# First feed-forward pass: order of casts, raw weight loads, residual loads and low parts, and two places for raw down-projection weights

## The reference, cut to what matters

```
xn = layer_norm(x, gamma)
h = xn @ Wff1                      # 512 -> 2 * 2048
a, gate = h[..., :2048], h[..., 2048:]
out = out + silu(gate) * a @ Wff2  # 2048 -> 512
x = x + tanh(g_xattn[0]) * out
```

## Time and profile before

| | us |
|---|---|
| median of 3 runs (2460.36 to 2461.43) | 2460.55 |
| the profiled execution | 2449.93 |
| its span in the trace | 2448.1 |
| TensorE matmul busy | 2133.0 (87%) |
| VectorE busy | 1324.5 (54%) |
| ScalarE busy | 674.0 (28%) |
| GpSimd busy | 621.1 (25%) |
| DMA, mean over the span | 231 GB/s |

### The profile page before, as it was taken

One profiled execution on the slowest core, in us unless ns is written; L12 is line 12 of the kernel. 1 busy time (PEld: TensorE's weight loads), 2 busy tenths in 40 slices (PEclk: granted clock), 3 DMA queues, 4 the chain that ended last, 5 costly groups with the idle time before them and its releaser, 6 DMA issues. The chain is left out here.

```text
span 2448.1 us, 30049 instructions
## 1 busy us (share of the span) xinstructions
PE 2133.0 (87%) x11425; PEld 1592.8 (65%) x11425; DVE 1324.5 (54%) x2112; ACT 674.0 (28%) x1066; POOL 621.1 (25%) x552
## 2 busy tenths in 40 slices
PE   6999999999968999999999999999897526434898
PEld 5677777776647778888888888887783102111577
DVE  7655666656325777666766676667661000000377
ACT  2544464446423332111111111222430000000231
POOL 5444564445337861330033000000220000000020
PEclk9999999999979999999999999999998767767999
DMA  4223213321186768774876484443769999999867
GB/s 153 75 100 126 83 61 110 125 82 57 39 327 223 254 215 334 260 235 168 316 247 226 156 332 184 155 156 133 291 242 407 426 432 425 421 429 426 320 226 255
DMA packets 181396, 565.13 MB, mean 231 GB/s; under 512 B 15472, under 2 KB 98960, under 8 KB 152560
## 3 DMA queue, kind: packets, MB, share of 16 engines
q1 hardware_dynamic: 171952, 504.37, 55.3%
q10 hardware_dynamic: 9312, 58.99, 5.8%
HBM read 450.07 MB, written 113.25 MB: 230 GB/s over the span
## 5 line engine op out<-in xcount | busy, mean ns | idle before, releaser
L1368 PE MATMUL ff_down<-w,u 128*128 128x512 f32 x1536 | 369.3, 397 | 15.8 <-DVE ff_x L1642 10.4
L1309 PE MATMUL ff_up<-ff_t,w 128*128 128x512 f32 x1488 | 358.9, 390 | 9.2 <-ACT ff_gate L1441 9.2
L1368 PEld LDWEIGHTS ff_down<-w,u 128*128 128x128 f32 x1536 | 289.3, 190 | 89.7 <-DVE ff_x L1642 24.4
L1309 PEld LDWEIGHTS ff_up<-ff_t,w 128*128 128x128 f32 x1488 | 280.0, 188 | 67.8 <-issue 9.6
L1309 PE MATMUL ff_up<-ff_b,w 128*128 128x512 f32 x1176 | 290.0, 391 | 14.8 <-DMA ff_b<-xnT 14.8
L1309 PEld LDWEIGHTS ff_up<-ff_b,w 128*128 128x128 f32 x1176 | 222.3, 189 | 61.6 <-issue 15.2
L1642 DVE SCALAR_TENSOR_TENSOR ff_x<-ff_down,gates,ff_x 128x512 f32<-128x512 f32 x256 | 190.5, 748 | 96.3 <-PE ff_down L1368 94.2
L2395 PE MATMUL e_down<-e_w,e_ug 128*32 128x512 f32 x480 | 70.3, 739 | 187.1 <-DMA e_w<-in_L_ffn_e_W 187.1
L2395 PEld LDWEIGHTS e_down<-e_w,e_ug 128*32 128x32 f32 x480 | 16.9, 133 | 239.2 <-DMA e_w<-in_L_ffn_e_W 196.2
L2067 POOL TENSOR_TENSOR yn_lo<-y,yn_hi 128x2048 fp32r<-128x2048 f32 x8 | 36.7, 4593 | 440.1 <-ACT yn_hi L2032 440.1
L2497 DVE TENSOR_TENSOR e_u_rows<-e_turned,e_b1T 128x128 f32<-128x128 f32 x16 | 4.7, 292 | 264.0 <-PE e_turned L2386 264.0
(11 more groups left out here) (441 smaller groups left out, 4204.2 us busy)
## 6 DMA issues: line engine op xcount, KB each, us to landing
w<-ff_w_factors SPq DMA_DIRECT2D x48, 1792.0 KB, 7.5
e_w<-in_L_ffn_e_W SPq DMA_DIRECT2D x17, 4096.0 KB, 23.4
e_wg<-in_L_ffn_e_Wg SPq DMA_DIRECT2D x16, 4096.0 KB, 35.6
e_w<-in_L_ffn_e_W ACTq DMA_DIRECT2D x13, 4096.0 KB, 53.0
ff_w_factors<-w SPq DMA_DIRECT2D x16, 1792.0 KB, 6.9
w<-ff_w_parts SPq DMA_DIRECT2D x48, 512.0 KB, 5.1
ff_t<-ff_t_factors SPq DMA_DIRECT2D x16, 1024.0 KB, 15.5
ff_b<-xnT SPq DMA_DIRECT2D x13, 1024.0 KB, 11.1
```

The lines of the kernel that those rows point to most:

```text
L1309: last = nc.tensor.matmul(bank[:, :], a, m, start=start and c == 0, stop=stop and c == 5)
L1368: last = nc.tensor.matmul(DN[m % 2][:, :], a, w, start=c == 0, stop=c == 5)
```

## The change

It touches only `feed_forward`.

- `raw2` and its semaphore become two each, place f % 2.
- SyncE: raw w2 1 is loaded right behind raw w2 0. Behind the factor loads the order becomes: raw 4 (after a wait for `w1_lo` of block 2), keep_w1(2), keep_w2(0), raw w2 2, keep_w1(0), the two x loads, raw 3 (after a wait for `w1_lo` of block 1 and for the first low parts), keep_w1(1), keep_w2(1), raw w2 3. In the loop raw f + 2 goes ahead of keep_w1(f), and raw w2 f + 1 is loaded in place of f.
- ScalarE: high_w2(1) goes ahead of group(1), high_s(1) behind group(2), and finish(2) ahead of high_a(3).
- GpSimd: make_w2(1) goes ahead of sum_w1(3).
- VectorE, in all passes: the residual of tile 2 goes between low_u(n, 1) and low_u(n, 0); the residuals behind `finish` begin with tile 3.

```diff
-        raw2 = mem.sbuf("ff_raw_w2", [P, D])
+        raw2 = [mem.sbuf(f"ff_raw_w2_{i}", [P, D]) for i in range(2)]
@@ sync
             load_raw2(0)
+            load_raw2(1)
             for i in (S2_T2, S1_T1, S3_T3, A22_T4):
                 load_factor(i, 0)
+            sp.wait_ge(w1_lo, step_of[2])
+            load_raw(4)
+            keep_w1(2)
+            keep_w2(0)
+            load_raw2(2)
+            keep_w1(0)
             x1_out, all_stores = x1_begun
             sp.wait_ge(x1_out, all_stores)
             for i in range(2):
                 load_x(0, i)
-            keep_w1(2)
-            load_raw(4)
-            keep_w2(0)
-            load_raw2(1)
-            keep_w1(0)
+            sp.wait_ge(w1_lo, step_of[1])
+            sp.wait_ge(first_lo, 3 * PLAIN)
+            load_raw(3)
             keep_w1(1)
-            load_raw(3)
             keep_w2(1)
-            load_raw2(2)
+            load_raw2(3)
             for f in range(3, FFQ):
-                keep_w1(f)
+                sp.wait_ge(w1_lo, step_of[f])
                 if 5 <= f + 2 < FFQ:
                     load_raw(f + 2)
+                keep_w1(f)
                 keep_w2(f - 1)
-                load_raw2(f)
+                if f + 1 < FFQ:
+                    load_raw2(f + 1)
                 pieces(1, f - 3)
@@ scalar
             high_w2(0)
+            high_w2(1)
             group(1, True)
             high_s(0)
+            group(2, True)
             high_s(1)
-            high_w2(1)
-            group(2, True)
+            finish(2)
             high_a(3)
             high_s(3)
             high_w2(2)
-            finish(2)
             high_a(4)
@@ gpsimd
             low_w1(1)
+            make_w2(1)
             sum_w1(3)
-            make_w2(1)
@@ vector, finish(n, g)
                 low_u(n, 1)
+                residual(g, [2])
                 low_u(n, 0)
@@ vector, behind each finish
-                    residual(g, range(2, TILES))
+                    residual(g, range(3, TILES))
```

More of the change, by code:

```diff
@@ L1127, in feed_forward @@
         raw_in = [mem.sem(f"ff_raw_in{i}") for i in range(2)]
-        raw2_in = mem.sem("ff_raw2_in")
+        raw2_in = [mem.sem(f"ff_raw2_in{i}") for i in range(2)]
         factor_in = [mem.sem(f"ff_factor_in{i}") for i in range(7)]
@@ L1166, in load_raw2 @@
             def load_raw2(f):
-                sp.dma_start(raw2[:, :], w2_v[f]).then_inc(raw2_in, 16)
+                sp.dma_start(raw2[f % 2][:, :], w2_v[f]).then_inc(raw2_in[f % 2], 16)
             def load_quarter(place, b, half, arrival):
@@ L1418, in high_w2 @@
             def high_w2(f):
-                act.wait_ge(raw2_in, 16 * (f + 1))
+                act.wait_ge(raw2_in[f % 2], 16 * (f // 2 + 1))
                 if f == 3:
@@ L1424, in high_w2 @@
                     act.wait_ge(w2_kept[f % 4], 16 * (f // 4))
-                nc.scalar.copy(w2[f % 4][:, 0, :], raw2[:, :]).then_inc(w2_hi, 1)
+                nc.scalar.copy(w2[f % 4][:, 0, :], raw2[f % 2][:, :]).then_inc(w2_hi, 1)
             def silu1(n):
@@ L1544, in make_w2 @@
                 pool.wait_ge(w2_hi, f + 1)
-                tt(w2[f % 4][:, 1, :], raw2[:, :], plain(w2[f % 4][:, 0, :]), ALU.subtract).then_inc(w2_lo, 1)
+                tt(w2[f % 4][:, 1, :], raw2[f % 2][:, :], plain(w2[f % 4][:, 0, :]), ALU.subtract).then_inc(w2_lo, 1)
             def make_piece(pair, i):
@@ L1663, in vector @@
             finish(2, 0)
-            residual(0, range(2, TILES))
+            residual(0, range(3, TILES))
             for pair in range(PAIRS):
@@ L1676, in vector @@
                     finish(n + 2 * c + 2, g + c)
-                    residual(g + c, range(2, TILES))
+                    residual(g + c, range(3, TILES))
                 group(n + FFQ - 3, False)
@@ L1682, in vector @@
                 if pair + 1 < PAIRS:
-                    residual(g + CHUNKS - 2, range(2, TILES))
+                    residual(g + CHUNKS - 2, range(3, TILES))
                     residual(g + CHUNKS - 1, range(0, 6))
@@ L1687, in vector @@
                     see_rows(2 * pair + 1)
-            residual(last_chunk - 2, range(2, 4))
+            residual(last_chunk - 2, range(3, 4))
             slot.first_statistics(dve)
```

## The result

| | before | after |
|---|---|---|
| median of the runs on one chip, us | 2460.36 (2452.14 to 2461.43, 5) | 2434.95 (2430.24 to 2439.38, 5) |
| ratio, 95% interval | | 0.9907 (0.9885 to 0.9929) |
| the profiled execution, us | 2449.93 | 2434.95 |
| its span, us | 2448.1 | 2433.2 |

The kernel became faster by 25.4 us between the medians; 25.2 had been forecast, and a time of 2435.4 against the measured 2434.95. The profiled executions differ by less, 15.0 us. To see which part belongs to the change, I cut each span at the feed-forward. Timeline of TensorE, before: the first product of the feed-forward, and the first down-projection product behind the last group of pass 4 (rows as in the groups above: start, length, what, idle before it).

What follows compares the result with a forecast made beforehand. Passes 2 to 4 were taken as bound by TensorE matmuls, with holes only at pass 1's head. Gains of 14.5 + 6.3 + 4.4 = 25.2 us off the median 2460.55 gave 2435.4 us, range 2430 to 2443.

Steps and rivals of the forecast that it cites:

- Part 1: Head of pass 1, group 2: TensorE's 9.24 us wait for silu0 of group 1 is removed; group 2 ends at 723.4.
- Part 2: Down-projection 0: make_w2(1) ends at 725.1, x lands at 728.3 (bound 736), down 0 ends at 737.4.
- Part 3: Group 3 of pass 1: raw block 3 lands at 732.0, group 3 starts at 740.0 instead of 755.97, 16.0 us.
- Part 4: Group 4 and down 1: 2.2 us lost to ScalarE's order; group 5 at 772.4 instead of 786.85, 14.5 us kept.
- Downs 2 to 7 of pass 1: Down-projections 2 to 7 lose 9.9 us; moving the third residual leaves 5.5, a gain of 4.4 us, bounds 2.5 to 7.
- Part 5: Third residual ahead of low_u(n,0): down-projections of passes 2 to 4 fall from 11.16 to 10.88, 6.3 us, bounds 0 to 7.
- Part 6: Remaining moves, raw blocks issued ahead of stores in the loop and new SyncE waits: no gain counted, price nothing.
- full gain: Rival, 0.12: down 1 loses nothing and down-projections reach 10.88 more often; 30 us gained, 2430.
- the x load as the new wait: Rival, 0.16: x lands at 736 and holds VectorE, group 3 starts only 9.4 us early; 2440.9.
- raw 3 landing as before: Rival, 0.08: raw block 3 still lands at 735.7, group 3 at 743.6; 10.9 + 10.7 kept, 2439.
- part 5 without effect: Rival, 0.07: the moved third residual gives nothing outside pass 1; 2441.7.

Runs made afterwards that it cites:

- e5: Kernel before with two places for raw w2 and the cast of w2 block 1 straight behind block 0's: 2452.4 us, ratio 0.9985, length 980.43.
- e3: Changed kernel with the two x loads put back ahead of raw block 4: 2434.47 us, ratio 0.9904 to before, length 960.49.
- e6: Changed kernel with make_w2(1) put back behind sum_w1(3) on GpSimd: 2444.81 us, ratio 0.9958 to before, length 967.68.
- e4: Changed kernel run again without an edit: 2432.94 us, ratio 0.9899 to before, length 960.58.
- e8: Changed kernel with block 5's casts moved behind group(4) on ScalarE in pass 1: 2436.99 us, ratio 0.9923 to before, length 960.92.
- e9: Changed kernel with the casts for blocks 5 and 6 moved behind finish(4) on ScalarE: 2428.72 us, ratio 0.9889 to before, length 957.24.
- e1: Kernel before with only the residual of tile 2 moved between the two low parts of u: 2446.14 us, ratio 0.9956, length 971.13.
- e2: Changed kernel with the residual of tile 2 put back behind both low parts: 2444.01 us, ratio 0.9945 to before, length 972.48.
- e12: As e11, with the casts of chunks 1 and 2 behind the finish on ScalarE: 2434.77 us, ratio 0.9912 to before, length 962.54.
- e7: Changed kernel with raw block 3 loaded behind the store of w1 block 1 again: 2436.71 us, ratio 0.9917 to before, length 964.09.
- e11: Changed kernel with the edits of e9 and e10 together: 2429.5 us, ratio 0.9880 to before, length 955.03.
- e10: Changed kernel with the store of w1 block 2 moved behind the load of raw block 3: 2432.77 us, ratio 0.9899 to before, length 958.47.

## Why the prediction was right, step by step

- **Part 1 (no wait for silu0), right.** TensorE no longer waits for silu0 (L1441, in after L1447) in group 2. E5 adds that the wait itself was worth nothing alone: the prediction did not count it as a gain of its own, and its working by start times was right in that.
- **Part 2 (down 0), right.** Forecast relative start 35.4, measured 36.5; x lands at 38.1 for 38.6, the low bound that I had taken. E3 shows that it held nothing. The gain comes from make_w2(1), 8.4 us (e6).
- **Part 3 (group 3), right in place.** Raw 3 landed at 43.1 for 42.3, group 3 started at 50.8 for 50.3: 15.5 us gained for 16.0. The clock fell behind down 0, as was held possible; I left its cost out because GpSimd was to set group 4. It did cost 1.8 us at group 4 (11.30 us from 743.39 to 754.69, for 9.52), and e4, at full clock, had group 5 no sooner (relative 88.3 for 87.5).
- **Part 4 (down 1), the term that was mis-sized.** Forecast: 2.2 us lost, group 5 at 82.7 relative, 14.5 kept (its own working, 759.5 + 10.88 + 2.2, gives 14.3). Measured: 5.1 us lost (15.95 less 10.88), group 5 at 87.5, **9.6 kept**. The mechanism was named (silus behind sums in ScalarE's order, VectorE's chain behind them), its size was wrong in two places. The thirteen operations of VectorE from silu1 of group 3 to the end of the first residual took 11.65 us without waits where I had taken 8.3 at 0.64 each, mostly by low parts beside GpSimd (2.30 us at 760.51), although that silu ended 1.1 us sooner than forecast (relative 65.3 for 66.4). And the second silu, of group 4 behind the next block's sums (767.83), was missing; VectorE waits 0.40 us more for it. Together they put the start of the third tile at relative 77.4 for 74.7, 2.7 us. The two are nearly level in after, so that either one taken away leaves most of the stand: e8 took the first silu away, and with it the long low parts, and the second silu held; e9 took both silus and the long low parts away, and down 1 was free. Another 2.0 us come behind the third tile's start: 10.1 us to group 5 for the 8.16 of 36 products, with stands of 1.03 and 0.17 us behind the low part of 2.22 us, and 0.8 us spread over these products at a granted clock of 1.00.
- **Downs 2 to 7 of pass 1, right in size.** 175.47 us from 780.17 to 955.64, less 170.0 of products, leave 5.5 lost for 9.9: 4.4 gained, as forecast. But by e1 (177.64) only about half of it belongs to the moved residual, and by e2 (179.72) next to nothing to the earlier head alone; the other half is theirs jointly. I had split the loss as 0.35 twice and 2.4 twice; it was 0.8, 2.4, 1.5 and 0.8.
- **Part 5, right.** All 18 single down-projections at 10.88: passes 2 to 4 gain 6.6 us, forecast 6.3; e1 confirms it alone.
- **Part 6, right**: nothing of it appears among TensorE's waits in 680 to 960.

```profile
PE ff_up L1315 <- DMA ff_b<-xnT: 15.0, 1, 15.0
PE ff_down L1374 <- DVE ff_x L1648: 7.5, 9, 2.9
PE ff_up L1315 <- POOL w L1546: 3.2, 1, 3.2
PE ff_down L1374 <- POOL w L1551: 3.1, 1, 3.1
```

**The sum.** 9.6 + 4.4 + 6.6 = 20.6 us, not 25.2. That the medians differ by 25.4 all the same does not bear the sum out to a microsecond: the interval is 17 to 28. The close hit of 2435.4 is luck in good part. Before's median in that comparison, 2460.36, was 3 to 4 us above its medians beside e1 to e12, and against the profiled execution the forecast (2424.7) missed by 10.2 us: 4.6 in the sum (4.9 in part 4, less 0.3 that part 5 gave more), 2.9 in the start and 2.8 behind. I had carried the 10.6 us between before's median and its profiled execution over as a constant; the rows put 5.7 us of it, against after, into stages outside the change, where that execution was quick. "The later stages are released by the end of the feed-forward, so nothing there gives it back" is not contradicted, as e1 to e12 show both longer and shorter ends without pattern, but a stage's own scatter of 7 us was not in the working. What makes that scatter is open. So is a difference between the two measures: for twelve of the thirteen changed kernels the medians lie further below before's than the lengths do, by 3.6 us in the mean of all thirteen. Whether before's one trace was short in the feed-forward too, no second trace of before tells.

The rivals: full gain failed at down 1; the x load as the new wait was refuted by e3, raw 3 landing as before by its landing at 43.1 for 46.0 and by e7; part 5 without effect by e1.

**A better version.** E11 has the shortest length, 4.3 us under after, and e9 the lowest median, 2428.72; both intervals overlap with after's, so that an advantage of about 0.2% is likely and not shown. As I read e11 and e12, the last 5 us in pass 1 need GpSimd's lead to be rebuilt before chunk 3, since putting the silus ahead only moves the place where it is missing; no run tried that.

## What to carry to other kernels

- Removing the largest wait gives nothing as long as the next operation that the bound engine waits for stays where it is (e5: 5.2 us less of one wait, 6.4 more of the next). Ask for the start time of the next consumer, not for the wait's length.
- When the bound engine becomes earlier, the slack of its helpers (the engines that prepare its operands) shrinks everywhere behind it. Every instruction on an in-order helper that stands behind a just-in-time producer must be listed, the second of a pair too; freeing one of two changes nothing (e8), and putting the consumer first takes the producer's inputs away (e11, e12).
- An edit that moves work on one helper also moves what runs beside the others (e9: GpSimd's stand shortened VectorE's low part). Look at both in the trace before calling either the cause.
- One profiled execution against another is uncertain by the scatter of all stages; the length of the stage that was changed is far sharper.

## What the runs showed of the hardware

- A VectorE 128x512 subtraction of two SBUF tensors took 0.68 us with GpSimd idle and 2.22 to 2.30 us beside GpSimd's 128x1024 subtraction, which itself took 2.68 and 2.79 instead of 2.40. In both cases it ended 0.55 us after GpSimd's (773.40 after 772.86, 762.81 after 762.26), so its price here hung on how long GpSimd's still ran. The residuals, which read PSUM and SBUF, stayed at 0.74 to 0.75 in the same stretch. The Trainium skill, "GPSIMD Engine Reference", section "8. Key points", says that GpSimd shares its SBUF interfaces with VectorE and that VectorE instructions with two SBUF inputs contend with it; the trace agrees, and gives the price here.
- TensorE's clock after a stand at GpSimd: a stand of 3.15 us was followed by 4.62 us for twelve products (granted clock 0.66, so part of the stretch at the lower of its levels, 1.2 and 2.4 GHz), one of 2.83 us of the same kernel (e4) by 3.01 us at 1.00, one of 7.36 (e7) by 4.98, mostly at the lower level (0.54). Ahead of down 0 of after, a stand of 3.08 us was followed by 48 products in 11.13 us, near the 10.88 of full clock. These few cases do not make a threshold.
- In SyncE's queue a load with a 1.84 MB store put ahead of it landed 4.7 us later relative to the first product (e7), but with another such store, issued 15 us earlier, taken from ahead of it only 1.3 us sooner (e10). As I read it, what counts is what is still in the queue when the load is issued.
